# Expert rows of a graph layer: added to the output by the scatter itself, in place of a second pass over all rows

## The chip, the cores and the metric

The kernel runs on one core of one Trainium2 chip. The metric is device time in microseconds. The kernel before was run three times: 5855.3, 5860.06 and 5858.4 us, median 5858.4.

## The reference

A layer of a graph network over 6250 nodes of 256 features and 106,250 directed edges (50,000 in both directions and a loop on each node). Two hypergraph convolutions, linear attention and a mixture of experts are added up:

```
xn = layernorm(x)
x  = x + gnn(xn, src, dst) + mix(xn)          # gnn: 2 x (gather by src, sum by dst; gather by dst, sum by src)
xf = layernorm(x)
logits = (xf * gamma + beta) @ Wr + br        # 8 experts, the best 2 of each node
w = softmax(the two highest logits)
for e in range(8):
    h = gelu(xn_ffn @ W1[e] + b1[e]);  y_e = h @ W2[e] + b2[e]
    y = y + y_e * w_full[..., e]              # 0 unless e is one of the node's two
out = x + y
```

What the change touches is the last part: each node has two expert rows, each to be multiplied by its weight and added to the node's row of `x`.

## The kernel before

All tiles have 128 partitions; nodes lie in NB = 49 blocks of 128 rows (the last has 106). The program is written engine by engine, in order, with semaphores between the queues.

**Sorting and four passes.** Edges are sorted on the chip. Then four passes (`gather_pass`, L597, and `product_pass`, L1558) each gather 831 chunks of 128 rows from a table in DRAM by indirect DMA from GpSimd, multiply each chunk by a one-hot matrix `ohg` on TensorE and add the result to its block on VectorE (L1070). In `product_pass` TensorE waits, once for each group of four chunks, until as many gather groups have arrived as a number in a register says (`arrived`, L1540); SyncE counts arrivals (`s_arr`).

**The node stage.** `by_group` works through 12 groups of four blocks and one of a single block: second weights, residual, normalisation, logits and the two best experts. SyncE stores the normalised rows to `xf_d` (L509). The finished `x` stays in SBUF (`accs[1]`).

**Assigning rows to chunks.** 12,500 pairs of node and expert are placed in chunks of 128 rows of one expert each. VectorE computes both softmax weights (`wt`, L1299) early in this stage and only needs them at the end. The chunk table is made by 98 small matmuls; from it come, for each slot, the node's row `tok`, the row of the result `dest`, and for each chunk its expert `eid`. `s_ready` is raised by L1350.

**The expert loop.** NCE = 108 chunks, in a hardware loop of 27 turns with ER = 4 chunks each. For each chunk:
- VectorE copies the chunk's column of `tok` (L1360), and GpSimd gathers the rows from `xf_d` (L644), up to four chunks ahead.
- TensorE transposes them (L1734), ScalarE copies the result to `xT` (L801), TensorE multiplies by W1 (`up`, L1740), VectorE adds b1 (L1364), ScalarE applies the gelu (L805).
- TensorE transposes `h` (L1757), ScalarE copies it to `hT` (L814), TensorE multiplies by W2 (the down product, L1764), VectorE adds b2 (L1383).
- GpSimd scatters the 128 rows to `ye_d` in DRAM (L655), which has a row for each pair. Slots with no pair go to rows behind these.

TensorE's order is: transpose of `h` of c, transpose of the rows of c+2, up of c+1, down of c. PSUM and SBUF buffers are doubled, the rings of gathered rows and of results have four places.

**The closing stage.** SyncE waits for all scatters, then loads `ye_d` back in 13 loads (L531), two buffers in turn. VectorE multiplies each of the two rows of a node by its weight and adds it to `x` (L1392), ScalarE's queue writes the output (L822, L824).

Of the kernel before, what the change touches and what calls it, by code (L numbers as in the profile page):

```python
# [48 lines left out]
def gps_layer(nc, x, src, dst, gnn_w1, gnn_b1, gnn_w2, gnn_b2, gnn_a, wqkv, wout, bout,  # L49
# [68 lines left out]
    NCE = -(-((2 * N + NE * (P - 1)) // P) // ER) * ER  # L118
# [10 lines left out]
    with ctx:  # L129
# [21 lines left out]
        xf_d = dram("xf_d", (NB * P, F))  # L151
        ye_d = dram("ye_d", (2 * NB * P + NCE * P, F))
# [78 lines left out]
        def column(o, f, c):  # L231

            if o == 0:
# [34 lines left out]
                    for at in (0, KT * 2 * INNER + 2 * PAIRS * F)]  # L268
# [15 lines left out]
        fs = sb("fs", [P, 800], f32)  # L284
# [3 lines left out]
                        "tok": ((NCE + ER,), i32), "dest": ((NCE,), i32),  # L288
                        "eid": ((NCE + ER,), i32), "tokb": ((ER,), i32), "destb": ((ER,), i32)})

        fb_ = carve(ohg_flat, {"pos": ((NK,), f32), "run": ((NK,), f32), "oh": ((NK,), f32), "chunk": ((NK,), f32),
                               "slot": ((NK,), f32), "ti": ((2, NK), i32), "code": ((NK,), i32), "w": ((4, NB), f32),
                               "wt": ((2, NB), f32), "val": ((NK,), f32), "code16": ((NK,), u16), "cnt": ((NE,), f32), "nch": ((NE,), f32), "nchi": ((2, NE), i32),
# [4 lines left out]
                               "dummy": ((NCE,), f32), "none": ((NCE,), f32), "a": ((NCE,), f32), "v": ((NCE,), f32),  # L298
                               "v16": ((NCE,), f16), "vi": ((NCE,), i32)})

        fe = carve(gbuf_flat, {"xg": ((ER, F), f32), "h": ((2, H), f32), "hT": ((2, H), f32), "y": ((ER, F), f32)})
        xT = carve(ohg_flat, {"xT": ((2, F), f32)})["xT"]
        yl = [gbuf_flat[:, n * 2 * G * F:(n + 1) * 2 * G * F].rearrange("p (b j f) -> p b j f", b=G, j=2) for n in range(2)]
# [32 lines left out]
         s_it, s_t1e, s_c1, s_up, s_b1, s_ge, s_t2, s_c2, s_dn, s_b2, s_yfreed, s_add, s_od) = [sem(n) for n in (  # L336
             "s_gt s_gtc s_u s_z s_v1 s_d1 s_fold s_shift s_xf s_xfd s_xfree s_xft s_xftc s_lg s_lgc "
             "s_ei s_ed s_ex s_ecnt s_etot s_eoh s_eused s_esort s_iw s_ready "
             "s_it s_t1e s_c1 s_up s_b1 s_ge s_t2 s_c2 s_dn s_b2 s_yfreed s_add s_od").split()]
        s_fl = [sem(f"s_fl{n}") for n in range(2)]  # L340
        s_ys = [sem(f"s_ys{k}") for k in range(ER)]
        s_yl = [sem(f"s_yl{k}") for k in range(2)]
# [54 lines left out]
        def _(sp):  # L397
# [108 lines left out]
            def store(q, par, n):  # L506
                sp.wait_ge(s_xf, q + 1)
                settle(sp)
                sp.dma_start(rows(xf_d, q * G, n), xh[par][:, 0:n, :]).then_inc(s_xfd, 16)  # L509
                sp.wait_ge(s_xfd, (q + 1) * 16)  # L510
                sp.sem_inc(s_xfree, 1)
# [5 lines left out]
            sp.sem_inc(s_yfreed, ER)  # L517
            with sp.Fori(0, NCE // ER) as i:
                for k in range(ER):
                    sp.wait_ge(s_ys[k], i * 16 + 16)  # L520
                    sp.sem_inc(s_yfreed, 1)
            for k in range(ER):
                sp.wait_ge(s_g[k], XG0 + 16 * (NCE // ER + 1))
            sp.wait_ge(s_ge, NCE + 1)

            for q in range(NG + 1):
                n = G if q < NG else 1
                m = P if q < NG else LAST
                if q >= 2:
                    sp.wait_ge(s_add, q - 1)  # L530
                sp.dma_start(yl[q % 2][0:m, 0:n, :, :], ye_d[q * G * 2 * P:q * G * 2 * P + n * 2 * m, :].rearrange("(b p j) f -> p b j f", p=m, j=2)).then_inc(s_yl[q % 2], 16)  # L531
# [4 lines left out]
        def _(pool):  # L536
# [101 lines left out]
            gp.iota(fd["dummy"], pattern=[[P, NCE]], base=2 * NB * P + 1, channel_multiplier=1, allow_small_or_imprecise_dtypes=True).then_inc(s_iw, 1)  # L638


            def gather(k, count):
                pool.wait_ge(s_it, count)
                settle(pool)
                gp.indirect_dma_start(fe["xg"][:, k, :], None, xf_d, bass.IndirectOffsetOnAxis(sm["tokb"][:, k:k + 1], 0)).then_inc(s_g[k], 16)  # L644
# [3 lines left out]
            for k in range(ER):  # L648
                gather(k, k + 1)
            with pool.Fori(0, NCE // ER) as i:  # L650
                for k in range(ER):
                    gather(k, i * ER + (ER + k + 1))
                    pool.wait_ge(s_b2, i * ER + (k + 3))
                    settle(pool)
                    gp.indirect_dma_start(ye_d, bass.IndirectOffsetOnAxis(sm["destb"][:, k:k + 1], 0), fe["y"][:, k, :], None).then_inc(s_ys[k], 16)  # L655
# [3 lines left out]
        def _(act):  # L659
# [139 lines left out]
            def copy_x(k, count):  # L799
                act.wait_ge(s_t1e, count)  # L800
                A(xT[:, k % 2, :], PS[:, k % 2, 0:F], ACT.Copy).then_inc(s_c1, 1)  # L801

            def gelu(k, count):
                act.wait_ge(s_b1, count)
                A(fe["h"][:, k % 2, :], fe["h"][:, k % 2, :], ACT.Gelu).then_inc(s_ge, 1)  # L805

            act.wait_ge(s_ready, 1)
            copy_x(0, 1)
            gelu(0, 1)
            copy_x(1, 2)  # L810
            with act.Fori(0, NCE // ER) as i:
                for k in range(ER):
                    act.wait_ge(s_t2, i * ER + (k + 1))
                    A(fe["hT"][:, k % 2, :], PS[:, 4 + k % 2, :], ACT.Copy).then_inc(s_c2, 1)  # L814
                    copy_x(k, i * ER + (k + 3))
                    gelu(k + 1, i * ER + (k + 2))


            for q in range(NG + 1):
                act.wait_ge(s_add, q + 1)  # L820
                if q < NG:
                    act.dma_start(rows(out, q * G, G), accs[1][:, q * G:(q + 1) * G, 0:F]).then_inc(s_od, 16)  # L822
                else:
                    act.dma_start(out[q * G * P:N, :], accs[1][0:LAST, q * G, 0:F]).then_inc(s_od, 16)  # L824
            act.wait_ge(s_od, 16 * (NG + 1))
# [3 lines left out]
        def _(dve):  # L829
# [468 lines left out]
            link(V.reciprocal(wt[:, 0, :], w[:, 2, :]))  # L1298
            link(TT(wt[:, 1, :], wt[:, 0, :], w[:, 1, :], ALU.mult))  # L1299
# [35 lines left out]
            dve.wait_ge(s_iw, 2)  # L1335
            v = fd["v"]
            link(V.tensor_copy(fd["v16"], PS[:, 1, 0:NCE]))
            link(V.tensor_copy(fd["vi"], fd["v16"].bitcast(u16)))
            link(TS(v, fd["vi"], float(-LOWEST), 0.0, ALU.add, ALU.max))
            link(TS(fd["none"], v, 0.0, None, ALU.is_equal))  # L1340
            link(V.memset(sm["tok"], 0))
            link(STT(out=fd["a"], in0=v, scalar=-1.0, in1=fd["none"], op0=ALU.add, op1=ALU.add))
            link(V.tensor_copy(sm["dest"], fd["a"]))
            link(TS(sm["tok"][:, 0:NCE], sm["dest"], 1, None, ALU.logical_shift_right))
            link(TT(fd["dummy"], fd["dummy"], fd["none"], ALU.mult))
            link(STT(out=sm["dest"], in0=v, scalar=-1.0, in1=fd["dummy"], op0=ALU.add, op1=ALU.add))
# [7 lines left out]
            def experts_of(i):  # L1354
                return nc.values_load_multi_w_load_instructions(
                    sm["eid"][0:1, ds(i * ER, ER + 1)], engines=(DVE,), min_val=0, max_val=NE - 1,
                    skip_runtime_bounds_check_because="computed on the chip as a minimum with NE - 1")[1]

            def token_numbers(k, w):
                V.tensor_copy(sm["tokb"][:, k:k + 1], sm["tok"][:, ds(w, 1)]).then_inc(s_it, 1)  # L1360

            def add_b1(k, count, e):
                dve.wait_ge(s_up, count)
                TT(fe["h"][:, k % 2, :], PS[:, 2 + k % 2, :], fa_["b1r"][:, ds(e, 1), :].rearrange("p a f -> p (a f)"), ALU.add).then_inc(s_b1, 1)  # L1364

            dve.wait_ge(s_fw2, 32)
            for k in range(ER):
                token_numbers(k, k)
            e0 = nc.values_load_multi_w_load_instructions(
                sm["eid"][0:1, 0:1], engines=(DVE,), min_val=0, max_val=NE - 1,  # L1370
                skip_runtime_bounds_check_because="computed on the chip as a minimum with NE - 1")[1][0]
            add_b1(0, 1, e0)
            with dve.Fori(0, NCE // ER) as i:
                es = experts_of(i)
                for k in range(ER):
                    w_ = i * ER + k
                    dve.wait_ge(s_t1e, w_ + 1)
                    token_numbers(k, w_ + ER)
                    add_b1(k + 1, w_ + 2, es[k + 1])
                    dve.wait_ge(s_yfreed, w_ + 1)  # L1380
                    V.tensor_copy(sm["destb"][:, k:k + 1], sm["dest"][:, ds(w_, 1)])
                    dve.wait_ge(s_dn, w_ + 1)
                    TT(fe["y"][:, k, :], PS[:, 6 + k % 2, 0:F], fr["b2r"][:, ds(es[k], 1), :].rearrange("p a f -> p (a f)"), ALU.add).then_inc(s_b2, 1)  # L1383


            for q in range(NG + 1):
                n, m = (G, P) if q < NG else (1, LAST)
                dve.wait_ge(s_yl[q % 2], 16 * (q // 2 + 1))
                for j in range(2):
                    for b in range(n):  # L1390
                        x2 = accs[1][0:m, q * G + b, 0:F]
                        a = STT(out=x2, in0=yl[q % 2][0:m, b, j, :], scalar=wt[0:m, j, q * G + b:q * G + b + 1], in1=x2,  # L1392
                                op0=ALU.mult, op1=ALU.add)
# [395 lines left out]
```

## Time and profile before

| | us |
|---|---|
| median of three runs | 5858.4 |
| the profiled execution | 5866.34 |
| its span, first to last instruction | 5864.6 |
| PE busy | 4113.0 (70%) |
| DVE busy | 3605.1 (61%) |
| ACT busy | 1255.1 (21%) |
| POOL busy | 3860.7 (66%) |
| mean granted TensorE clock | 0.868 |

The busy shares are averages over stages with different limits. The four passes lie between about 650 and 5006 us, the node stage and the assignment between there and 5320, the expert loop from 5321 to 5787, the closing stage behind it. All times below are us from the span's start. Matmul ends are modelled. The clock is given as a share of full speed.

### The profile page before, as it was taken

What the parts mean: (1) busy time and instruction counts of PE and PEld (TensorE: products, weight loads), DVE (VectorE), ACT (ScalarE), POOL (GpSimd) and SP (SyncE); (2) the same over time, 40 slices, a digit from 0 to 9 for tenths busy, and PEclk for the clock granted to TensorE, in tenths of its full rate; (3) what the DMA queues carried; (4) which work ended last, traced back from release to release, by engine and by line L of the source; (5) the groups of instructions that cost most, each with busy time, mean ns of one, the idle gap of its engine ahead of it and who ended that gap; (6) DMA issues with size and microseconds to landing.
All of it is one profiled execution on the core that took longest, in us unless ns stands there. A gap on an engine that the chain in (4) does not pass through costs nothing.

```text
span 5864.6 us, 68260 instructions
## 1 busy us (share of the span) xinstructions
PE 4113.0 (70%) x16858; PEld 2694.3 (46%) x16859; DVE 3605.1 (61%) x11329; ACT 1255.1 (21%) x3285; POOL 3860.7 (66%) x3972
## 2 busy tenths in 40 slices
PE   4799799999975776777465555555566555557994
PEld 2555466665643444444344334333434434444662
DVE  7788788888876666566755554574555554454324
ACT  0388455555520000000100000000000000222331
POOL 2777777777776777777477777767777777003442
PEclk9899899999998999999787887887787777768997
DMA  3400233333334333333344444444333333411125
GB/s 123 133 2 2 59 100 102 102 100 101 100 104 137 112 112 112 113 112 111 112 139 136 136 140 137 136 143 142 105 105 106 105 105 105 134 53 41 63 64 161
DMA packets 322692, 616.69 MB, mean 105 GB/s; under 512 B 79716, under 2 KB 199096, under 8 KB 321848
## 3 DMA queue, kind: packets, MB, share of 16 engines
q0 software_dynamic: 182400, 464.97, 27.8%
q1 hardware_dynamic: 127932, 133.60, 6.9%
q10 hardware_dynamic: 12028, 14.28, 0.7%
q8 instruction: 137, 2.24, 0.2%
q14 instruction: 195, 1.60, 0.1%
HBM read 525.55 MB, written 87.01 MB: 104 GB/s over the span
## 4 chain that ended last, share of the span: by engine, by line
PE 40%; DVE 15%; DMA 14%; issue 10%; POOL 8%; SPq 1%; ACT 1%; DVEq 1%; ACTq 0%; PEldq 0%; POOLq 0%; PEld 0%
PE PS L1558 19%; POOL rowset L597 8%; PE PS L1482 7%; DVE rowset L1070 7%; DMA rowset<-table,idx 7%; PE PS L1740 3%; PE PS L1764 3%; PE PS L1596 3%; DMA region<-xn_d 2%; DMA skip_d<-region 2%; DVE ohg L1079 2%; PE PS L1634 2%; DMA region<-xt_d 1%; PE PS L1757 1%; DMA rowset<-ye_d 1%
## 5 line engine op out<-in xcount | busy, mean ns | idle before, releaser
L597 POOL DMA_INDIRECT rowset<-table,idx x3324 | 3206.0, 964 | 1088.3 <-issue 706.1
L1558 PE MATMUL PS<-rowset,ohg 128*128 x7040 | 2074.4, 437 | 925.1 <-issue 335.0
L1070 DVE TENSOR_TENSOR rowset<-rowset,PS 128x257 f32 (+1 forms) x3520 | 1478.0, 420 | 1482.0 <-PE PS L1558 1461.5
L1558 PEld LDWEIGHTS PS<-rowset,ohg 128*128 128x128 f32 x7040 | 1436.8, 215 | 1567.7 <-issue 1358.7
L1079 DVE TENSOR_SCALAR ohg<-iota,dl 128x128 f32<-128x128 f16 x2640 | 793.9, 301 | 91.7 <-issue 91.7
L1482 PE MATMUL PS<-region 128*128 128x416 f16 x3328 | 653.3, 339 | 0.0
L605 POOL DMA_INDIRECT scattered_d<-rowset x384 | 372.2, 969 | 132.9 <-issue 121.3
L1482 PEld LDWEIGHTS PS<-region 128*128 128x128 f16 x3328 | 324.5, 98 | 256.9 <-issue 0.9
L692 ACT ACTIVATE region<-region 128x128 f16<-128x128 f16 x832 | 334.1, 402 | 453.9 <-DVE region L994 431.7
L993 DVE TENSOR_SCALAR region<-iota_c,region 128x832 f16<-128x832 f16 x832 | 380.5, 457 | 22.9 <-issue 22.7
L693 ACT ACTIVATE region<-region 128x128 f16<-128x128 f16 x832 | 321.0, 386 | 0.0
L1482 PE MATMUL PS<-rowset,region 128*128 128x416 f16 x1792 | 320.3, 340 | 0.0
L1596 PE MATMUL PS<-region 128*128 128x512 f32 x392 | 234.8, 730 | 117.0 <-DMA region<-xt_d 117.0
L761 ACT ACTIVATE region<-region 128x8 f32<-128x8 f32 x2 | 0.5, 294 | 1377.8 <-PEq L1406 1377.8
L1634 PE MATMUL PS<-gmat,region 128*128 128x256 f32 x196 | 97.2, 648 | 246.1 <-DMA region<-xn_d 246.1
L993 DVE TENSOR_SCALAR rowset<-iota_c,region 128x832 f16<-128x832 f16 x448 | 227.4, 508 | 42.5 <-PE PS L1482 42.2
L1482 PEld LDWEIGHTS PS<-rowset,region 128*128 128x128 f16 x1792 | 174.6, 97 | 146.0 <-issue 2.1
L655 POOL DMA_INDIRECT ye_d<-rowset,fs x108 | 106.3, 984 | 199.4 <-DVE fs L1360 143.2
L725 ACT ACTIVATE region<-PS 128x1024 f32<-128x1024 f32 x49 | 50.1, 1023 | 842.2 <-PEq L1406 842.2
L994 DVE TENSOR_SCALAR region<-iota_h,region 128x128 f16<-128x128 f16 x832 | 214.5, 258 | 0.0
L1740 PE MATMUL PS<-region,ohg 128*128 x436 | 207.9, 600 | 0.0
L1764 PE MATMUL PS<-rowset 128*128 x864 | 204.1, 379 | 0.0
(322 smaller groups left out, 3530.2 us busy)
## 6 DMA issues: line engine op xcount, KB each, us to landing
rowset<-table,idx POOLq DMA_INDIRECT x3324, 2.8
table<-rowset SPq DMA_DIRECT2D x21, 896.0 KB, 5.1
region<-xt_d SPq DMA_DIRECT2D x98, 128.0 KB, 2.2
rowset<-ye_d SPq DMA_DIRECT2D x12, 1024.0 KB, 7.5
xpad_d<-rowset SPq DMA_DIRECT2D x1, 6272.0 KB, 20.7
xn_d<-rowset SPq DMA_DIRECT2D x49, 128.0 KB
xt_d<-rowset SPq DMA_DIRECT2D x49, 128.0 KB
table<-rowset SPq DMA_DIRECT2D x49, 128.0 KB
```

Source lines behind the costliest of these rows:

```text
L597: gp.indirect_dma_start(rowset[:, at + c % ring, 0:F], None, tables[p], bass.IndirectOffsetOnAxis(idx[p % 2][:, c:c + 1], 0)).then_inc(s_g ...
L605: gp.indirect_dma_start(scattered_d, bass.IndirectOffsetOnAxis(ln["place"][:, c:c + 1], 0), ln["edge"][:, c:c + 1], None).then_inc(s_sc[h] ...
L692: A(ohv[:, k % RING, 0, :], ohs[o][:, k % RING, :], ACT.Copy, scale=column(o, 2, c))
L693: A(ohv[:, k % RING, 1, :], ohs[o][:, k % RING, :], ACT.Copy, scale=column(o, 3, c)).then_inc(s_ohs[o], 1)
L993: TS(ohc[o][:, k % RING, :], iota_c[:, 0:NC], column(o, 0, c), None, ALU.is_equal)
L1070: TT(a, a, chunk_sum(p, k), ALU.add).then_inc(s_acc[p], 1)
L1079: m = TS(ohg[:, k % U, :], iota_1[:, :], dl[p % 2][:, i * U + k:i * U + k + 1], None, ALU.is_equal)
L1482: m = MM(PS[:, 2 * f + h, 0:HC], ohv[:, k % RING, f, :], ohc[o][:, k % RING, h * HC:(h + 1) * HC], start=False, stop=False)
L1558: m = MM(chunk_sum(p, k), ohg[:, k, :], rowset[:, ds(slot_of[k], 1), 0:width(p)].rearrange("p a f -> p (a f)"), start=True, stop=True)
L1596: MM(PS[:, h, :], mx["xt"][:, kt, :], mx["wkv"][:, kt, h * INNER:(h + 1) * INNER], start=kt == 0, stop=kt == KT - 1)
L1740: m = MM(PS[:, 2 + k % 2, :], xT[:, k % 2, kt * P:(kt + 1) * P], fr["w1"][:, ds(e, 1), kt, :].rearrange("p a f -> p (a f)"), start=kt == 0 ...
L1764: m = MM(PS[:, 6 + k % 2, 0:F], fe["hT"][:, k % 2, t * P:(t + 1) * P], fa_["w2"][:, ds(es[k], 1), t, :].rearrange("p a f -> p (a f)"), sta ...
```

## The change

- The second result buffer `ye_d` and the closing stage are gone.
- SyncE writes the finished `x` to `out` right behind the last store of `xf_d`, while rows are assigned to chunks.
- The rows of `xf_d` are two words longer (FW = 258), and SyncE writes both weights of each node there, from `wt`, now laid out as pairs. GpSimd's first gather waits for that. A gathered row brings both weights with it.
- VectorE picks the weight by whether the slot holds the node's first or second expert (`first`, `second`), in two operations per chunk. ScalarE multiplies the result by it, a fourth operation per chunk.
- GpSimd's scatter goes to `out` and adds. Slots with no pair have a row number beyond the last node and are left out. Since two chunks can hold the same node, each scatter waits until the one before has landed.
- The loop has 105 chunks and is written out; `tok` and `dest` are read in place, without the copies to `tokb` and `destb`. Expert numbers are read for 16 chunks at a time (17 registers) in place of four (5 registers).
- In `product_pass` the number of arrivals waited for is made at least 1 by one register operation for each group of four chunks (its declared minimum is 0 instead of 1).

```diff
-    NCE = -(-((2 * N + NE * (P - 1)) // P) // ER) * ER
+    NCE = (2 * N + NE * (P - 1)) // P
+    FW = F + 2
...
-        xf_d = dram("xf_d", (NB * P, F))
-        ye_d = dram("ye_d", (2 * NB * P + NCE * P, F))
+        xf_d = dram("xf_d", (NB * P, FW))
...
             by_group(sp, load, lambda q, par, n: None, store)
...
-            for k in range(ER):
-                sp.wait_ge(s_g[k], XG0 + 16 * (NCE // ER + 1))
-            sp.wait_ge(s_ge, NCE + 1)
-            for q in range(NG + 1):
-                n = G if q < NG else 1
-                m = P if q < NG else LAST
-                if q >= 2:
-                    sp.wait_ge(s_add, q - 1)
-                sp.dma_start(yl[q % 2][0:m, 0:n, :, :], ye_d[...]).then_inc(s_yl[q % 2], 16)
+            for q in range(NG + 1):
+                if q < NG:
+                    sp.dma_start(rows(out, q * G, G), accs[1][:, q * G:(q + 1) * G, 0:F]).then_inc(s_od, 16)
+                else:
+                    sp.dma_start(out[q * G * P:N, :], accs[1][0:LAST, q * G, 0:F]).then_inc(s_od, 16)
+            sp.wait_ge(s_wts, 1)
+            sp.dma_start(xf_d[:, F:FW].rearrange("(b p) j -> p b j", p=P), fb_["wt"]).then_inc(s_wtd, 16)
+            sp.wait_ge(s_od, 16 * (NG + 1))
             for k in range(ER):
+                sp.wait_ge(s_ys[k], 16 * -(-(NCE - k) // ER))
...
+            def gather(c):
+                if c >= ER:
+                    pool.wait_ge(s_t1e, c - ER + 1)
+                    pool.wait_ge(s_wsel, c - ER + 1)
+                gp.indirect_dma_start(fe["xg"][:, c % ER, :], None, xf_d, bass.IndirectOffsetOnAxis(sm["tok"][:, c:c + 1], 0)).then_inc(s_g[c % ER], 16)
...
+            pool.wait_ge(s_wtd, 16)
+            for c in range(ER):
+                gather(c)
+            pool.wait_ge(s_od, 16 * (NG + 1))
+            for c in range(NCE):
+                if c + ER < NCE:
+                    gather(c + ER)
+                pool.wait_ge(s_scl, c + 1)
+                if c:
+                    pool.wait_ge(s_ys[(c - 1) % ER], 16 * ((c - 1) // ER + 1))
+                gp.indirect_dma_start(out, bass.IndirectOffsetOnAxis(sm["dest"][:, c:c + 1], 0), fe["y"][:, c % ER, :], None,
+                                      bounds_check=N - 1, oob_is_err=False, compute_op=ALU.add).then_inc(s_ys[c % ER], 16)
...
+            for c in range(NCE):
+                act.wait_ge(s_t2, c + 1)
+                A(fe["hT"][:, c % 2, :], PS[:, 4 + c % 2, :], ACT.Copy).then_inc(s_c2, 1)
+                if c + 2 < NCE:
+                    copy_x(c + 2)
+                if c + 1 < NCE:
+                    gelu(c + 1)
+                act.wait_ge(s_b2, c + 1)
+                A(fe["y"][:, c % ER, :], fe["y"][:, c % ER, :], ACT.Copy, scale=sm["wsel"][:, 1, c % ER:c % ER + 1]).then_inc(s_scl, 1)
...
+            def weights(c):
+                at = c % ER
+                dve.wait_ge(s_t1e, c + 1)
+                if c >= ER:
+                    dve.wait_ge(s_scl, c - ER + 1)
+                link(TS(sm["wsel"][:, 0, at:at + 1], fe["xg"][:, at, F + 1:FW], sm["second"][:, c:c + 1], None, ALU.mult))
+                STT(out=sm["wsel"][:, 1, at:at + 1], in0=fe["xg"][:, at, F:F + 1], scalar=sm["first"][:, c:c + 1],
+                    in1=sm["wsel"][:, 0, at:at + 1], op0=ALU.mult, op1=ALU.add).then_inc(s_wsel, 1)
...
+                weights(c)
+                if c + 1 < NCE:
+                    add_b1(c + 1, es[c % U + 1])
+                if c >= ER:
+                    dve.wait_ge(s_ys[c % ER], 16 * (c // ER))
+                dve.wait_ge(s_dn, c + 1)
+                TT(fe["y"][:, c % ER, :], PS[:, 6 + c % 2, 0:F], fr["b2r"][:, ds(es[c % U], 1), :].rearrange("p a f -> p (a f)"), ALU.add).then_inc(s_b2, 1)
...
                         if k % IB == 0:
-                            pe.wait_ge(s_arr[p], arrived[k // AG])
+                            pe.reg_alu(at_least, pe.to_reg(arrived[k // AG]), 1, ALU.max)
+                            pe.wait_ge(s_arr[p], at_least)
```

GpSimd's queue in the expert loop, before: gathers of `xf_d` and scatters to `ye_d` in turn, the gather behind VectorE's copy of the row numbers (`s_it`), the scatter behind VectorE's bias add (`s_b2`).

```order
L644 DMA rowset<-xf_d,fs 128x256 [waits s_it]
L653 REGISTER_ALU
L655 DMA ye_d<-rowset,fs 26368x256 [waits s_b2]
L642 REGISTER_ALU
L644 DMA rowset<-xf_d,fs 128x256 [waits s_it]
```

The same place in the changed kernel, from the first gather on. `s_wtd` is the store of the weights, `s_od` the writes of `out`, `s_scl` ScalarE's scale, `s_ys0` to `s_ys3` the landings of scatters.

```order
L636 DMA rowset<-xf_d,fs 128x258 [waits s_wtd,s_xfree,s_ready]
L636 DMA rowset<-xf_d,fs 128x258 x3
L636 DMA rowset<-xf_d,fs 128x258 [waits s_wsel,s_t1e,s_od]
L650 DMA out<-rowset,fs 6250x256 [waits s_scl]
L636 DMA rowset<-xf_d,fs 128x258 [waits s_wsel,s_t1e]
L650 DMA out<-rowset,fs 6250x256 [waits s_ys0,s_scl]
L636 DMA rowset<-xf_d,fs 128x258 [waits s_wsel,s_t1e]
L650 DMA out<-rowset,fs 6250x256 [waits s_ys1,s_scl]
```

The order of gathers and scatters is kept; each scatter but the first has gained the wait for the landing of the one before it, and it waits for ScalarE instead of VectorE.

ScalarE's queue in the expert loop, before: copy of `hT` (L814), of `xT` (L801), gelu (L805).

```order
L811 ISA
L814 ACTIVATE rowset<-PS 128x512 [waits s_t2]
L800 REGISTER_ALU
L801 ACTIVATE ohg<-PS 128x256 [waits s_t1e]
L804 REGISTER_ALU
L805 ACTIVATE rowset<-rowset 128x512 [waits s_b1]
L814 ACTIVATE rowset<-PS 128x512 [waits s_t2]
```

The same place in the changed kernel (L809, L797 and L801 are the same three operations).

```order
L809 ACTIVATE rowset<-PS 128x512 [waits s_t2]
L797 ACTIVATE ohg<-PS 128x256 [waits s_t1e]
L801 ACTIVATE rowset<-rowset 128x512 [waits s_b1]
L815 ACTIVATE rowset<-rowset,fs 128x256 [waits s_b2]
L809 ACTIVATE rowset<-PS 128x512 [waits s_t2]
```

The scale L815, which waits for the bias add behind the down product of c, stands ahead of the copy of `hT` of chunk c+1.

## Rows read from the trace of the kernel before

**Rows 1.** Windows: length, busy us by engine (instructions), granted clock, DMA share, GB/s.

```profile
5500.00:5600.00 100.00, 100.00 (x435) 67.58 (x434) 30.31 (x97) 36.14 (x73) 46.71 (x48) 1.00 0.20 63
5800.00:5865.00 65.00, 0.00 (x0) 0.00 (x0) 35.81 (x86) 0.00 (x0) 0.00 (x0) 0.50 0.78 262
```

**Rows 2.** The chain that ended last, from 5770 on: start us, us, what.

```profile
5776.64 1.73 PE PS L1764 x8
5780.80 1.74 PE PS L1764 x8
...
5783.17 3.13 issue
...
5786.52 2.45 DMA ye_d<-rowset,fs
...
5789.35 5.32 DMA rowset<-ye_d
```

**Rows 3.** Timeline, the last DMA issued.

```profile
5860.20 0.28 ACTq L824 DMA_DIRECT2D out<-rowset  x1
```

**Rows 4.** Timeline in the expert loop: start us, us, engine, line [idle before, releaser].

```profile
5504.69 0.38 ACT L801 ACTIVATE ohg<-PS 128x256 f32<-128x256 f32 x1
...
5505.51 0.19 PEld L1764 LDWEIGHTS PS<-rowset 128*128 128x128 f32 x1 [0.24 <-issue]
5505.93 1.89 PE L1764 MATMUL PS<-rowset 128*128 x8
...
5506.25 0.69 DVE L1364 TENSOR_TENSOR rowset<-PS,rowset 128x512 f32<-128x512 f32 x1 [1.95 <-PE PS L1740]
5506.36 0.96 POOL L644 DMA_INDIRECT rowset<-xf_d,fs  x1 [0.30 <-issue]
...
5507.66 0.66 PE L1757 MATMUL PS<-ident,rowset 128*128 128x128 f32 x4
5507.98 0.42 DVE L1383 TENSOR_TENSOR rowset<-PS,region 128x256 f32<-128x256 f32 x1 [0.98 <-PE PS L1764]
...
5508.36 0.60 ACT L814 ACTIVATE rowset<-PS 128x512 f32<-128x512 f32 x1 [0.75 <-PE PS L1757]
...
5509.23 0.99 POOL L655 DMA_INDIRECT ye_d<-rowset,fs  x1 [1.91 <-DVE fs L1360]
```

**Rows 5.** Timeline ahead of the expert loop: the weights, the last preparation, the first gather.

```profile
5264.25 0.21 DVE L1299 TENSOR_TENSOR ohg<-ohg 128x49 f32<-128x49 f32 x1
...
5320.01 0.22 DVE L1350 TENSOR_SCALAR fs<-rowset 128x112 int32<-128x112 f32 x1
...
5321.34 0.97 POOL L644 DMA_INDIRECT rowset<-xf_d,fs  x1 [6.42 <-DVE fs L1360]
```

**Rows 6.** SyncE's DMAs by line (ns min/median/max, first and last start), then by issue.

```profile
L509 SPq DMA_DIRECT2D xf_d<-rowset x13: 345/396/406, 5043.5 to 5250.7; - x13
...
DMA to landing us min/median/max: 1.7/3.1/3.6
...
L490 SPq DMA_DIRECT2D region<-in_L_ffn_Wr x1: 613/613/613, 3965.5 to 3965.5; - x1
...
L492 SPq DMA_DIRECT2D region<-in_L_ffn_beta x1: 2526/2526/2526, 3968.3 to 3968.3; - x1
...
xpad_d<-rowset SPq DMA_DIRECT2D x1, 6272.0 KB, 20.7
```

**Rows 7.** DMA issues from 5345 to 5760: count, median us from issue to landing.

```profile
rowset<-xf_d,fs POOLq DMA_INDIRECT x100, 2.8
ye_d<-rowset,fs POOLq DMA_INDIRECT x100, 2.4
```

**Rows 8.** By line: TensorE's queue in the passes, and GpSimd's gathers, 700 to 1740 us.

```profile
L1535 PEldq TENSOR_LOAD <-blk_row x220: 1101/1104/1769, 659.5 to 4985.3; - x110
...
L1558 PEldq FUSED_REGOPS  x3520: 46/46/46, 665.5 to 5003.6; - x196
...
L597 POOL DMA_INDIRECT rowset<-table,idx x791 | 799.4, 1011 | 241.0 <-issue 171.8 <-DVE rowset L1070 69.1
```

More of the change, by code:

```diff
@@ L283, in gps_layer @@
         NK = 2 * NB
-        fs = sb("fs", [P, 800], f32)
+        fs = sb("fs", [P, 900], f32)
         sm = carve(fs, {"inv": ((G,), f32), "stats": ((G, 6), f32), "mv": ((G, 2), f32), "rstd": ((5, G), f32), "nega": ((1,), f32),
@@ L508, in store @@
                 settle(sp)
-                sp.dma_start(rows(xf_d, q * G, n), xh[par][:, 0:n, :]).then_inc(s_xfd, 16)
+                sp.dma_start(xf_d[ds(q * G * P, n * P), 0:F].rearrange("(b p) f -> p b f", p=P), xh[par][:, 0:n, :]).then_inc(s_xfd, 16)
                 sp.wait_ge(s_xfd, (q + 1) * 16)
@@ L637, in _ @@
             gp.iota(fd["iw"], pattern=[[1, NCE + ER]], base=0, channel_multiplier=0, allow_small_or_imprecise_dtypes=True).then_inc(s_iw, 1)
[L638 to L644, printed above, removed]
+            def gather(c):
[3 more added lines that the diff above has]
+                gp.indirect_dma_start(fe["xg"][:, c % ER, :], None, xf_d, bass.IndirectOffsetOnAxis(sm["tok"][:, c:c + 1], 0)).then_inc(s_g[c % ER], 16)
             pool.wait_ge(s_ready, 1)
             pool.wait_ge(s_xfree, 2 + NG + 1)
[L648 to L655, printed above, removed]
+            pool.wait_ge(s_wtd, 16)
[10 more added lines that the diff above has]
+                                      bounds_check=N - 1, oob_is_err=False, compute_op=ALU.add).then_inc(s_ys[c % ER], 16)
         @block.scalar
@@ L796, in _, with copy_x, gelu @@
             A(fb_["w"][:, 1, :], fb_["w"][:, 0, :], ACT.Exp).then_inc(s_ex, 1)
[L799 to L805, printed above, removed]
-            act.wait_ge(s_ready, 1)
[L808 to L825, printed above, removed]
+            def copy_x(c):
+                act.wait_ge(s_t1e, c + 1)
+                A(xT[:, c % 2, :], PS[:, c % 2, 0:F], ACT.Copy).then_inc(s_c1, 1)
+            def gelu(c):
+                act.wait_ge(s_b1, c + 1)
+                A(fe["h"][:, c % 2, :], fe["h"][:, c % 2, :], ACT.Gelu).then_inc(s_ge, 1)
+            act.wait_ge(s_ready, 1)
+            copy_x(0)
+            gelu(0)
+            copy_x(1)
+            for c in range(NCE):
[7 more added lines that the diff above has]
+                A(fe["y"][:, c % ER, :], fe["y"][:, c % ER, :], ACT.Copy, scale=sm["wsel"][:, 1, c % ER:c % ER + 1]).then_inc(s_scl, 1)
         @block.vector
@@ L1362, in add_b1 @@
-            def add_b1(k, count, e):
-                dve.wait_ge(s_up, count)
-                TT(fe["h"][:, k % 2, :], PS[:, 2 + k % 2, :], fa_["b1r"][:, ds(e, 1), :].rearrange("p a f -> p (a f)"), ALU.add).then_inc(s_b1, 1)
-            dve.wait_ge(s_fw2, 32)
[L1367 to L1383, printed above, removed]
@@ L1386, in _, with add_b1 @@
[L1386 to L1393, printed above, removed]
-                    if j == 0:
-                        link(a)
-                a.then_inc(s_add, 1)
+            def add_b1(c, e):
+                dve.wait_ge(s_up, c + 1)
+                TT(fe["h"][:, c % 2, :], PS[:, 2 + c % 2, :], fa_["b1r"][:, ds(e, 1), :].rearrange("p a f -> p (a f)"), ALU.add).then_inc(s_b1, 1)
@@ new lines, in _ @@
+            dve.wait_ge(s_fw2, 32)
+            for c in range(NCE):
+                if c % U == 0:
+                    es = experts_of(c)
+                if c == 0:
+                    add_b1(0, es[0])
+                weights(c)
[5 more added lines that the diff above has]
+                TT(fe["y"][:, c % ER, :], PS[:, 6 + c % 2, 0:F], fr["b2r"][:, ds(es[c % U], 1), :].rearrange("p a f -> p (a f)"), ALU.add).then_inc(s_b2, 1)
```

109 lines of the change are left out of this document (51 added, 58 removed).

## The prediction

> **What bounds the kernel now.** I read the busy shares of the last stretches first, then the chain of work that ended last, then one turn of the expert loop instruction by instruction, and last the DMA landings. The windows show two regimes. From 5500 to 5600 us TensorE is busy 100.00 of 100 us at clock 1.00. From 5800 to the end TensorE, ScalarE and GpSimd do nothing, VectorE is busy 35.81 of 65 us and the DMA engines 0.78 [rows 1]. That is the closing stage, in which the expert rows come back from `ye_d`, are weighted, added and written. The chain says where it begins: the last down product ends at 5780.80 + 1.74 = 5782.54, the last scatter goes out at 5786.52 and lands at 5788.97, and the first of 13 loads of `ye_d` starts at 5789.35 [rows 2]. The span is 5864.6, so 75.6 us lie behind the last landing. The last DMA is issued at 5860.20 [rows 3], 4.4 us before the end.
>
> The expert loop turns in 4.16 us per chunk: the down product starts at 5776.64 and again at 5780.80 [rows 2]. All its PE work is back to back.
>
> **What goes.** The closing stage, and three chunks: 3 x 4.16 = 12.5 us. The 3.13 us of issue ahead of the last scatter [rows 2] are mostly a hitch of that one turn, since a scatter normally starts 0.83 us behind VectorE (5507.98 + 0.42 = 5508.40, then 5509.23) [rows 4].
>
> **What comes at the loop's start.** VectorE's last preparation ends at 5320.23, the first gather starts at 5321.34 because four copies stand between [rows 5]. They go, and GpSimd starts 0.83 behind: 5321.06. A second iota that VectorE waited for goes too, and one small operation of the chain: together I take 0.6 us earlier, within 0 and 1.
>
> The new gate on that gather is the store of the weights. The last store of `xf_d` is issued at 5250.7 [rows 6]; those stores land in 1.7 us at the least [rows 6], so the 13 writes of `out` start at about 5253. The 6.3 MB store of rows of 1 KB landed in 20.7 us, so they drain by about 5274 [rows 6]. The weights themselves are ready at 5264.46 [rows 5]. Behind the writes stands one DMA of 128 x 49 = 6272 pieces of 8 bytes. The nearest rows are two loads of 256 small pieces each: SyncE was held 613 ns by one and 2526 ns by the other [rows 6], 2.4 and 9.9 ns a piece, so 15 to 62 us, landing at 5289 to 5336. I take 25 us, which is near the shorter (the longer stood behind megabytes of other loads): it lands near 5300, 20 us before it is needed. The upper end costs 16 us.
>
> The Trainium skill ("DMA: Bandwidth & Descriptors", section "Rules for kernel authors") says that a non-contiguous last dimension becomes one descriptor per element; pairs of 8 bytes are close to that case, and by it this small store is as dear as 6272 pieces. The trace of before has no such store.
>
> **The loop, engine by engine.** TensorE's matmuls are the same, so its floor stays 4.16 us. ScalarE gets a fourth operation, scale 128x256. It stands behind the gelu and ahead of the next copy of `hT`, and waits for VectorE's bias add, which ends at 5508.40. The copy would have started at 5508.36 [rows 4]. The nearest ScalarE row of that width takes 0.38 us (128x512: 0.60) [rows 4]; I take 0.42. So the scale runs 5508.45 to 5508.87 and the copy 5508.90 to 5509.50. The weight load that needs it starts one period behind 5505.51, at 5509.67 [rows 4]: 0.17 us are left. Cost 0; if the scale took 0.60, or the wait more, up to 0.3 x 104 = 31 us. VectorE's two 128x1 operations need less than 0.22 each (a 128x112 one takes 0.22 [rows 5]) and fall in its idle time ahead of the next b1 add (1.95 us before 5506.25 [rows 4]), where a copy went out: 0.
>
> GpSimd is where the change can hurt. Scatter c now waits for the landing of scatter c-1 as well as for the scale, and behind it in the queue stands the gather of c+5, for which TensorE has chunks of reserve. A plain scatter lands 2.4 us after it starts (2.45 in the chain), and GpSimd starts 0.83 behind its release. The gather (0.30 + 0.96) [rows 4] fits in the flight. So the serial chain turns in 2.45 + 0.83 = 3.28 us with a plain write; 4.16 - 3.28 = 0.88 us is the room for what the adding costs, which I call x.
>
> x is in no row of before. From below: 0, if reading the old rows overlaps with all else. From near: a gather, which reads DRAM, lands in 2.8 us and a scatter in 2.4 [rows 7], so a DRAM read adds 0.4; and the DMA engines are busy 0.20 of the time on one gather and one scatter per turn [rows 1], 0.83 us, so 0.42 us for another 128 rows: x = 0.8. From above: a whole gather's flight ahead of the write, 2.8 - 0.96 = 1.84, and the building of the descriptors twice as long, + 0.98 [rows 4]: x = 2.8. I take 0.8, since the two reads have no cause to wait for each other: the chain turns in 4.1 us, just under TensorE's 4.16.
>
> The Trainium skill ("Collectives: The Full Stack", section "The bandwidth ceiling: the fold count and why AG ≠ RS ≠ AR") says that an adding DMA is slow because it reads two sources and not because of the addition, and measured half a copy's rate. By it the data part of a scatter doubles, which is the 0.42 above; no row of before shows it.
>
> **Register work.** Each group of four chunks in the four passes gets one more register operation on TensorE's queue: 880 x 46 ns = 40 us if nothing hid it [rows 8]. It stands behind the wait for the one-hots and ahead of the wait for arrivals. The gathers set the pace even in the first pass, where TensorE is busiest: 791 gathers take 799.4 us and the 241.0 us between them are the same 0.30 us that lies between any two [rows 8], so GpSimd never waits for TensorE: 0. Expert numbers are read 17 at a time, 7 times, instead of 5 at a time. A read of 16 in the passes takes 1.10 us [rows 8], and TensorE was 100% busy across such reads every four chunks: 0.
> By the Trainium skill ("Runtime: NRT & Kernel Launch", section "Instruction fetch mechanics") a register read costs about 200 ns per register, thus 3.4 us a read; beyond a down product's 1.73 us it would stall TensorE 1.7 us six times, 10 us. The trace's 1.10 us for 16 speaks against it.
>
> **The sum.** Last down product ends 5782.54 - 12.5 - 0.6 = 5769.4. VectorE's add: + 0.15 + 0.44 = 5770.0; scale + 0.47; GpSimd + 0.83 = 5771.3; landing + 2.45 + 0.8 = 5774.6. The end: 4.4 us behind the last issue of before, of which 1.7 was landing if the 106 rows took the least that a store of `xf_d` does [rows 6], so + 2.7 = 5777.3. That is 87.3 us under the span of 5864.6. The profiled execution took 5866.34, 7.9 over the median of 5858.4; carried over to the median: 5858.4 - 87.3 = 5771.
>
> **The rivals.** What a run of this kernel can tell from no change is 0.2%, 11.7 us.
> - Forecast, 0.48: x up to 0.88, the chain of scatters hides behind TensorE. 5771, by itself 5762 to 5780 (start, end, a few tenths per turn).
> - The scatters set the pace, but less than the tail gives back, 0.25: x = 1.3, 4.58 us a turn, 104 x 0.42 = 44 us more: 5815. For it: 0.08 us of room is little. Against: nothing else is on the DMA engines.
> - Slower than before, 0.22: the wait of scatter c for the landing of scatter c-1. It decides from x = 1.83 on: (87.3 + 11.7) / 104 = 0.95 over 4.16. With x = 2.8 the turn is 6.08 us, 104 x 1.92 = 200 us more: 5971. For it: the rows would be read, added and written in series, 8 per DMA engine. Against: gathers of the passes land in 2.8 us with several in flight.
> - The chain hides, but the weights land late (+16) or ScalarE's order holds up TensorE (+31), 0.05: 5787 to 5802. That ScalarE has only 0.17 us left speaks for it.
>
> No change within 0.2% needs x between 1.61 and 1.83: 0.05, taken out of the second. Faster: 0.48 + 0.20 + 0.05 = 0.73; slower 0.22. The range runs from 5762 to 5900 (a turn of 5.4 us, x = 2.1), which leaves out about 0.05 below and 0.14 above.
>
> **What will show it.** Right: down products 4.16 us apart and TensorE at 100%; adding scatters landing in under 3.3 us from their start; first gather near 5320.7; the last scatter near 5771 and the end some 6 us behind; register work without a trace in the gather rate. Wrong: the bias add of chunk c waiting for a DMA, TensorE idle each turn, scatters back to back with their landings (the second and third case); GpSimd waiting at the first gather for the weights' store; TensorE waiting for ScalarE's copy of `hT`.

## The result: 0.27% faster where 1.5% was forecast

The changed kernel took 5851.4 us (median of 15 runs, 5841.9 to 5862.4), the kernel before, run beside it, 5864.5 us (5855.3 to 5872.7). The ratio is 0.9973, 95% interval 0.9967 to 0.9980. That is 13 us less between the medians and 16 by the ratio, where 87 were forecast. The changed kernel's profiled execution took 5854.1 us, its span is 5851.6 at a mean clock of 0.870.

The closing stage is gone as forecast; the expert loop gave most of it back. First the windows, with the columns of [rows 1].

```profile
5500.00:5600.00 100.00, 90.82 (x376) 57.93 (x375) 30.20 (x84) 39.96 (x84) 53.60 (x42) 1.00 0.34 54
...
5800.00:5851.00 51.00, 35.10 (x146) 22.75 (x145) 12.10 (x33) 15.42 (x31) 21.83 (x17) 0.93 0.25 34
```

TensorE's full 100 us have become 90.82, and GpSimd issues 42 DMAs instead of 48 in the same time. The loop turns more slowly. The scatter's own line says why: ns min/median/max and first and last start, then what GpSimd's idle time ahead of it ended with (us, times), then the landing.

```profile
L650 POOL DMA_INDIRECT out<-rowset,fs x105: 1554/1586/1652, 5347.4 to 5842.8; - x105
...
  DMA out<-rowset,fs: 157.4, 85
...
  ACT rowset L815: 36.5, 15
...
DMA to landing us min/median/max: 2.7/3.8/4.9
```

An adding scatter keeps GpSimd for 1.59 us where the plain one took 0.99 [rows 4], and lands 3.8 us behind its start instead of 2.4 [rows 7]. The profile puts 85 of 105 waits down to a DMA of the scatter's own kind, the landing of the scatter before. From first to last start there are 495.4 us, over 104 turns 4.764 us each, against 4.16. Two turns in the chain (start us, us, what):

```profile
5506.23 0.52 ACT rowset L815
5506.75 0.12 issue
5506.88 3.91 DMA out<-rowset,fs
...
5510.90 0.55 issue
...
5511.67 3.89 DMA out<-rowset,fs
```

The scatter's landing takes 3.91 us, and the next one starts 0.88 us behind it. The timeline shows how TensorE comes to wait (start us, us, engine, line [idle before, releaser]):

```profile
5501.56 0.51 ACT L815 ACTIVATE rowset<-rowset,fs 128x256 f32<-128x256 f32 x1 [1.25 <-DVE rowset L1375]
...
5502.17 1.59 POOL L650 DMA_INDIRECT out<-rowset,fs  x1 [2.71 <-ACT rowset L815]
...
5504.06 0.98 POOL L636 DMA_INDIRECT rowset<-xf_d,fs  x1 [0.30 <-issue]
...
5506.87 0.44 PE L1716 MATMUL PS<-ident,rowset 128*128 128x128 f32 x2 [0.83 <-DMA rowset<-xf_d,fs]
5506.88 1.59 POOL L650 DMA_INDIRECT out<-rowset,fs  x1 [1.84 <-ACT rowset L815]
5508.77 0.98 POOL L636 DMA_INDIRECT rowset<-xf_d,fs  x1 [0.30 <-issue]
```

Each gather stands behind a scatter in GpSimd's queue. As the scatters fall back, so do the gathers; after the reserve of some chunks is used up, TensorE's transpose of the rows (L1716) waits for a gather, 61.4 us in all between 5380 and 5820:

```profile
POOL out L650 <- DMA out<-rowset,fs: 135.7, 74, 2.2
...
PEld PS L1716 <- DMA rowset<-xf_d,fs: 61.4, 85, 2.4
```

The rows that name `ACT rowset L815` as a scatter's releaser, at 5502.17 and 5506.88 and in the chain, are put down wrongly. There are 105 scales and 105 scatters, in the same order, so they can be paired by counting. The scatter at 5506.88 is the 34th, and its scale, also the 34th, ended at 5502.08 (the row of 5501.56), 4.8 us earlier; the scale that ended at 5506.75 belongs to the next scatter. What ended 0.88 us before 5506.88 is the landing of the scatter of 5502.17. Counted so over the whole loop, no scatter but the first starts within 1.3 us of the end of its own scale (median 4.3 us), and 94 of 104 start 0.88 us behind the landing before. In the scatters' chain there is nothing else: the 495.4 us are 399.8 of flights, start to landing, and 95.7 from a landing to the next start. The lag behind the own scale grows from 0.85 us at the first chunk to 5.1 at the ninth, and that is the reserve being used up.

The end of the program: the last scatter and GpSimd's drain, changed kernel.

```profile
5842.82 1.55 POOL L650 DMA_INDIRECT out<-rowset,fs  x1 [1.99 <-DMA out<-rowset,fs]
```

```profile
L130 POOLq DRAIN  x1: 8798/8798/8798, 5842.6 to 5842.6; - x1
```

The last scatter landed at 5845.52. The drain lasts until 5851.40, 7.0 us beyond the end of that instruction, and every engine waits for it. The same drain in the kernel before took 2.9 us and ended at 5789.3, in the shadow of the closing stage:

```profile
L129 POOLq DRAIN  x1: 2926/2926/2926, 5786.4 to 5786.4; - x1
```

**The account against the forecast span of 5777.3.** 74.3 us are to be found. The 104 turns are 495.4 - 432.9 = 62.5 us longer. The first scatter starts at 5347.4 where 5771.3 - 432.9 (104 x 4.162) = 5338.4 was forecast: 9.0. From the last scatter's start to the end there are 8.8 us where 5.95 were forecast: 2.9.

### The profile page after: what moved, and what is told of

Its sections match the earlier page's. It is cut to its first block, busy times and chain, and to the rows that moved or that the text cites. A ratio compares the mean times of both kernels' runs of the same rounds, so it can differ in the third digit from the quotient of the medians.

```text
span 5851.6 us, 67858 instructions
## 1 busy us (share of the span) xinstructions
PE 4131.0 (71%) x16796; PEld 2689.7 (46%) x16796; DVE 3583.2 (61%) x11213; ACT 1292.3 (22%) x3378; POOL 3922.4 (67%) x3961
## 4 chain that ended last, share of the span: by engine, by line
DMA 22%; PE 22%; POOL 15%; DVE 15%; issue 12%; DVEq 1%; ACT 1%; SPq 1%; ACTq 0%; POOLq 0%; PEldq 0%; PEld 0%
POOL rowset L590 15%; PE PS L1540 12%; DMA rowset<-table,idx 10%; DVE rowset L1060 7%; DMA out<-rowset,fs 6%; PE PS L1461 4%; PE PS L1578 2%; DMA region<-xn_d 2%; DMA skip_d<-region 2%; PE PS L1616 2%; DVE ohg L1069 1%; DMA region<-xt_d 1%; PE PS L1673 1%; DVE ohg L1064 1%; DVEq L1060 0%
## 5 line engine op out<-in xcount | busy, mean ns | idle before, releaser
L650 POOL DMA_INDIRECT out<-rowset,fs x105 | 166.5, 1586 | 206.6 <-DMA out<-rowset,fs 157.4
L1351 DVE TENSOR_TENSOR rowset<-PS,rowset 128x512 f32<-128x512 f32 x105 | 72.7, 693 | 227.7 <-PE PS L1722 227.7
```

## The experiments

Kernels beside which the same time of the kernel before stands shared a chip.

**The changed kernel again**, for the same chip as the next three (before: 5874.9 us there).

> The changed kernel again, beside the runs of before that the next three kernels share. Both theories on the loop expect 0.997 of before. Of the 13 us by which its passes ended later in the profile: if they belong to the kernel, the last gather of the passes ends near 5013 again and pass 0 takes about 1101 us again; if they are scatter between executions, the last gather ends anywhere from 4998 to 5014.

Measured 5862.0 us, ratio 0.9978 (0.9969 to 0.9987): the result stands. In its profile the first pass takes 1101.0 us and the last gather of the passes ends at 5012.2, much as in the first profile of this kernel (1101.5 and 5013.6).

**The adding taken out of the scatter.** The sum is left out: rows overwrite each other.

```diff
-  bounds_check=N - 1, oob_is_err=False, compute_op=ALU.add)
+  bounds_check=N - 1, oob_is_err=False)
```

> The changed kernel with a scatter that overwrites in place of one that adds (the sum is left out); all waits, the row filter, the scale and the order stay. Theory: the added cost of the adding DMA, 1.35 us of landing, sets the turn; without it the chain of scatters turns in about 3.3 us, the loop falls back to TensorE's 4.16 us, the scatter lands in 2.45 us and the kernel takes 60 us less than the changed one (about 5790). Rival, ScalarE's fourth operation and its order set the turn: it stays at 4.7 us and the time at 5851. Rival, the filter of row numbers is the cost: GpSimd's instruction stays at 1.59 us and about half of the gain is missing (turn near 4.2 to 4.3).

Measured 5801.6 us, ratio 0.9869 (0.9854 to 0.9885), 60 us under the changed kernel beside it. The window and the scatter's line:

```profile
5500.00:5600.00 100.00, 99.34 (x429) 66.80 (x427) 34.96 (x96) 45.41 (x96) 47.24 (x49) 1.00 0.21 62
```

```profile
L650 POOL DMA_INDIRECT out<-rowset,fs x105: 983/1017/1035, 5359.7 to 5793.6; - x105
...
  ACT rowset L815: 182.9, 95
...
DMA to landing us min/median/max: 2.1/2.5/3.5
```

With every wait left in place, the plain write takes 1.02 us, lands in 2.5, and seldom holds up the next: the releaser is ScalarE 95 times (97 scatters start 0.8 us behind their own scale, paired by counting), and the turn is (5793.6 - 5359.7) / 104 = 4.172 us. So it takes the price of adding to slow the loop; the wait for a landing, ScalarE's fourth operation and the longer rows don't do it without that. The price has two parts: 1.59 - 1.02 = 0.57 us for the instruction, and (3.8 - 1.59) - (2.5 - 1.02) = 0.73 us behind it.

**Two targets in turn.** Even chunks are added into `out`, odd ones into a second tensor, so a scatter waits only for the last but one. The final sum of the two is left out.

```diff
-  if c:
-      pool.wait_ge(s_ys[(c - 1) % ER], 16 * ((c - 1) // ER + 1))
-  gp.indirect_dma_start(out, ...
+  if c >= 2:
+      pool.wait_ge(s_ys[(c - 2) % ER], 16 * ((c - 2) // ER + 1))
+  gp.indirect_dma_start((out, out2)[c % 2], ...
```

> The changed kernel with two target tensors: even chunks add to the output, odd chunks to a second tensor that starts with the same rows (the final sum of the two is left out), so that a scatter waits for the landing of the one before the last. Theory, the wait for the neighbour's landing sets the turn and nothing else: adding scatters still take 1.59 us on GpSimd and land in 3.8 us, yet the loop turns in 4.16 to 4.2 us, TensorE is at 100% and the time is about 5800 where the changed kernel has 5862 on that chip (ratio to before 0.987). Rival, the adding itself is the limit (reads of DRAM, the DMA engines): the turn stays above 4.6 us and the landings grow beyond 4 us as two overlap.

Measured 5789.8 us beside 5859.7 of the kernel before, ratio 0.9874 (0.9857 to 0.9890).

```profile
5500.00:5600.00 100.00, 100.00 (x435) 67.43 (x434) 35.10 (x97) 45.60 (x97) 62.17 (x49) 1.00 0.40 63
```

```profile
L656 POOL DMA_INDIRECT out<-rowset,fs x105: 1555/1587/1652, 5361.0 to 5794.3; - x105
...
DMA to landing us min/median/max: 2.7/3.8/4.4
```

The adding scatter is as long as ever (1.59 and 3.8 us), yet TensorE is at 100 of 100 and the turn 4.167 us. The length of the scatter does harm only through the wait for the neighbour's landing.

**Without the row filter.** Slots with no pair add into rows behind the nodes of a scratch tensor, so that no row is filtered (`bounds_check` gone). Expert rows don't reach the output.

```diff
-  gp.indirect_dma_start(out, ..., bounds_check=N - 1, oob_is_err=False, compute_op=ALU.add)
+  gp.indirect_dma_start(acc_d, ..., compute_op=ALU.add)
```

> The changed kernel adding into a scratch tensor that has rows for the empty slots, so that no filter of row numbers is needed (the output is left without its expert rows). Theory, the adding makes the longer building of descriptors, not the filter: 1.55 to 1.59 us as in the changed kernel, turn 4.7 us, time within 5 us of the changed one; the three chunks at the end, mostly empty slots, no longer turn faster (3.5 to 3.9 before), which costs 2 to 3 us. Rival, filter and adding together make it: the instruction falls by 0.1 us or more and the turn with it, 10 us over the loop.

Measured 5841.2 us beside 5859.7, ratio 0.9967 (0.9957 to 0.9977).

```profile
L656 POOL DMA_INDIRECT acc_d<-rowset,fs x105: 1554/1586/1644, 5342.9 to 5830.0; - x105
...
DMA to landing us min/median/max: 3.6/3.8/5.3
```

The instruction stays at 1.59 us, so its 0.57 us are the adding's. The turn is not quite the same, and here the rival was right in part: it is 4.684 us on average (487.1 us over the loop) against 4.764 (495.4). In the chain of this run:

```profile
5558.43 3.83 DMA acc_d<-rowset,fs
...
5563.04 3.83 DMA acc_d<-rowset,fs
```

The next scatter starts at 5563.04, 0.78 us behind the landing at 5562.26, where it takes 0.88 with the filter (both are the usual value of their runs). The filter brings a register move ahead of each scatter (`L650 POOLq MOVE` x105), which this kernel doesn't have. So the filter costs no flight and no instruction time of the adding scatter, but about 0.1 us of its start, some 10 us over the loop, part of which the last chunks give back: with the filter, chunks of empty slots land in 2.7 us. A plain scatter took 0.99 us before and 1.02 above; the two differ in their target as well.

**The wait only where it is needed.** Within one expert no node comes twice, so neighbouring chunks can share a node only where the expert changes. SyncE waits for the last but one always, for the last with a number computed on the chip (`need`: 16 more where the expert changes), and then releases GpSimd.

```diff
+  link(TT(fd["chg"], fd["ew"][:, 1:NCE + 1], fd["ew"][:, 0:NCE], ALU.not_equal))
+  link(STT(out=sm["need"], in0=fd["chg"], scalar=16.0, in1=fd["iy"][:, 0:NCE], op0=ALU.mult, op1=ALU.add))
...
+  for c in range(1, NCE):                                   # SyncE
+      if c >= 2:
+          sp.wait_ge(s_ys[(c - 2) % ER], 16 * ((c - 2) // ER + 1))
+      if c > ER:
+          sp.reg_alu(landed_before, sp.to_reg(need[(c - ER - 1) % U]), 1, ALU.max)
+          sp.wait_ge(s_ys[(c - 1) % ER], landed_before)
+      else:
+          sp.wait_ge(s_ys[(c - 1) % ER], 16 * ((c - 1) // ER + 1))
+      sp.sem_inc(s_go, 1)
...
-  pool.wait_ge(s_ys[(c - 1) % ER], 16 * ((c - 1) // ER + 1))
+  pool.wait_ge(s_go, c)
```

> The changed kernel, but a scatter waits for the landing of the one before it only where the expert changes (two chunks of one expert hold no node twice), and always for the one before that; SyncE does the waiting, against a number computed with the chunk table, and releases GpSimd. Theory: 98 of 104 turns fall to TensorE's 4.16 us, 60 us less than the changed kernel, ratio to before 0.987 (0.986 to 0.990). Rival, TensorE's turn was bound by the gathers that stand behind the scatter in GpSimd's queue and not by the wait: turn above 4.5 us, and a gain of less than 20 us.

Measured 5787.9 us beside 5859.7, ratio 0.9877 (0.9860 to 0.9893): 72 us less than before, with the whole output computed.

```profile
5500.00:5600.00 100.00, 99.80 (x431) 67.00 (x431) 34.94 (x96) 45.28 (x96) 62.16 (x49) 1.00 0.40 63
```

```profile
L668 POOL DMA_INDIRECT out<-rowset,fs x105: 1552/1588/1649, 5343.8 to 5777.3; - x105
...
  SPq L538: 20.3, 11
...
DMA to landing us min/median/max: 2.7/3.8/4.2
```

11 of 104 waits are put down to SyncE's release, where in the changed kernel all 104 scatters started behind a landing; the turn is 4.168 us. In the timeline two adding scatters stand closer than a landing:

```profile
5499.38 1.59 POOL L668 DMA_INDIRECT out<-rowset,fs  x1 [2.09 <-issue]
...
5502.65 1.59 POOL L668 DMA_INDIRECT out<-rowset,fs  x1 [0.40 <-issue]
```

5502.65 is 3.27 us behind 5499.38. This form, which the changed kernel forbids itself, lets a late chunk catch up.

**The register operation.** The passes ended 13.3 us later than before, so it was put into the kernel before alone, and made five in the changed one.

```diff
-  pe.wait_ge(s_arr[p], arrived[k // AG])
+  pe.reg_alu(at_least, pe.to_reg(arrived[k // AG]), 1, ALU.max)
+  pe.wait_ge(s_arr[p], at_least)
```

> The kernel before with the one register operation per group of four chunks and nothing else of the change. If register work is what the passes lost: 10 to 15 us more than before, ratio 1.002, and the last gather of the passes ends near 5013. If gathers set the pace and it is hidden: ratio 1.000 within 0.001, last gather near 5000, and each of the four passes within 2 us of before.

> The changed kernel with five register operations in place of one for each of the 880 groups. If they lie on the path: 4 x 880 x 46 ns = 160 us more than the changed kernel. If gathers set the pace: the same time as the changed kernel in passes 1 to 3, and at most a few us in pass 0 where TensorE is 95% busy.

One operation in the kernel before: 5882.1 us beside 5874.9, ratio 1.0014 (1.0005 to 1.0023). Five in the changed kernel: 5861.2 us, ratio 0.9980 (0.9971 to 0.9989), the same as with one (0.9978). One costs about 7 us, four more nothing. With one, the last gather of the passes ends at 5019.2. On another chip (before: 5865.8 us) one and five were put into the kernel before side by side.

> The kernel before with one register operation per group, a second time, on another chip, beside the kernel with five. If the 0.14% belong to it: 1.0010 to 1.0018 again. If it was scatter between executions: within 0.001 of 1. The last gather of the passes then ends wherever pass 0, with its number of long gathers, puts it.

> The same with five operations per group. On the slow chip this was 0.9999 of before, with 0.9987 to 1.001 as interval. If the time of the operations counts at all, it is above the kernel with one by up to 4 x 880 x 46 ns = 160 us, ratio 1.03; if it is hidden, both kernels are equal within 0.001.

1.0011 (1.0000 to 1.0021) for one, 1.0010 (1.0001 to 1.0019) for five. So it isn't the time of the operations. The edit also lowers the declared minimum of the number, and no run parts this from the operation. Whether its place matters was asked on a chip where the kernel before took 7378.7 us, so only ratios can be read: the operation ahead of the wait for the one-hots, five of them in the old place, and the kernel with the wait at the change of expert with the early operation.

> The kernel before with the one register operation per group, placed ahead of the wait for the one-hots, so that the three waits of a group stand on one instruction again as before. If the parted waits made the 0.14% of the register operation alone, this is 1.000 of before within 0.001. If the operation itself did, it is 1.0014 again.

> The kernel before with five register operations per group. If each operation costs its 46 ns on the path, even a fifth of the time: 1.0014 + 0.0055 = 1.007. If what costs is only that there is an operation between the two waits, or the code around it: 1.0014 again. If the 0.14% of one operation was scatter of the executions: anywhere from 0.9995 to 1.002.

> The kernel that waits for the neighbour's landing only where the expert changes, with the register operation placed early. Loop as there (4.16 us a turn). If the placing counts: 0.9863 of before; if not: 0.9877 again.

Ratios 1.0007 (0.9994 to 1.0020), 0.9999 (0.9987 to 1.0011) and 0.9885 (0.9863 to 0.9906). The first two can't be told from each other, from no change, or from the 1.0010 above, and the third repeats the gain of 0.9877 on a slower chip. On this chip GpSimd's gathers waited 1080.2 us for VectorE's adds (305.2 in the kernel before), so another thing sets the pace there and the first two say little about the other chips. Place and mechanism of the operation stay open.

## Why the prediction was wrong, step by step

**The step that failed: x, the cost of adding, taken as 0.8 us.** It is 1.3 (0.57 + 0.73, by the run without adding) to 1.4 (3.8 - 2.4). The forecast took from the nearest rows only the reading of the old rows, and argued that "the two reads have no cause to wait for each other". It left the longer instruction (+ 0.98, there a part of the upper bound) out of the likeliest value. A part of either kind came: 0.57 us of a longer instruction, 0.73 behind it. The decision hung on 0.08 us of room between 4.08 and 4.16, and the case "x up to 0.88" was less than a third of the way from 0 to 2.8, so nothing in the rows carried a chance of 0.48. The chain is 3.8 + 0.88 = 4.7 us, the usual turn. Eight turns of 5.4 to 6.1 and four of 3.5 to 4.0 make the mean 4.764. Of the eight, four stand behind a landing that took 4.6 to 4.9 us, and in four the next scatter started 1.6 to 2.2 us behind the landing instead of 0.88; what caused either is open.

The second rival was the right one: x = 1.3, 4.58 us a turn, 5815. Its turn was still short by 0.18 us, 19 us over 104: half is the flight (3.84 on average against 3.75), half the start behind a landing (0.92 against 0.83). With the 9.0 ahead of the loop and the 2.9 at the end that makes 5846. The last 5 us are the carrying over: the profiled execution of before lay 7.9 us over the median used, that of the changed kernel only 2.7.

**The Trainium skill's rule on the adding DMA** ("Collectives: The Full Stack", section "The bandwidth ceiling: the fold count and why AG ≠ RS ≠ AR") puts the cost into reading two sources. The run without adding fits it in part: 0.73 us of 1.3 lie behind the instruction, where the prediction had 0.42 for the data, but 0.57 lie in the instruction itself, on GpSimd. No run parts the reading from the addition.

**The passes: register work at 0, measured about 7 us.** The gathers' rate was the argument. By line, GpSimd from 700 to 1740 us in the changed kernel, as in [rows 8]:

```profile
L590 POOL DMA_INDIRECT rowset<-table,idx x784 | 800.2, 1021 | 240.7 <-issue 179.5 <-DVE rowset L1060 61.2
```

784 gathers instead of 791 in the same time: in this stretch seven gathers, at 1040 / 791 = 1.31 us each 9 us, went missing. The idle time between gathers is 0.31 us as before (240.7 / 784), so GpSimd still doesn't wait for TensorE; the gathers themselves are longer, 1021 ns on average instead of 1011. Of the 13.3 us by which the last gather comes later, 1.3 lie ahead of the first pass, 6.4 in it (1101.5 us from first to last gather, against 1095.1), 1.6 in the third, 4.0 between passes. The second and fourth are equal to within 0.3 us. In the first pass some gathers start 2.3 us apart instead of 1.3: 33 of them before, 38 now, and 33 to 46 in the ten profiles with the operation on chips of the usual speed, whose first pass took 1098.2 to 1111.9 us. Of the kernel before there is only one such profile. So a part of the 13.3 us is chance of that execution; the ratios of the three runs that add only this to the kernel before (1.0014, 1.0011, 1.0010) give 6 to 8 us. That the gathers' rate hides all register work was thus wrong by a little: the rate itself fell. What stretches those few gathers isn't settled.

**The start.** The first gather, forecast near 5320.7, came 11.2 us later:

```profile
5331.47 0.22 DVE L1340 TENSOR_SCALAR fs<-rowset 128x109 int32<-128x109 f32 x1
...
5331.96 0.97 POOL L636 DMA_INDIRECT rowset<-xf_d,fs  x1 [5.45 <-DVE fs L1340]
```

13.3 us come from the passes. Behind them it was 2.7 us quicker than before, where 0.6 was forecast: GpSimd starts 0.27 us behind VectorE, not 0.83. From the first gather to the first scatter it took 15.4 us, where 17.7 were forecast, so of the 11.2 us 9.0 are left. The store of the weights did what was forecast:

```profile
5264.83 14.64 SPq L517 DMA_DIRECT2D out<-rowset  x12
...
5280.77 1.22 SPq L521 DMA_DIRECT2D xf_d<-ohg  x1
```

It landed at 5294.95, forecast near 5300, needed at 5332: 6272 pieces of 8 bytes within 14.2 us. The number is partly luck: the writes of `out` started at 5264.8 and not at 5253, and the small store took 14.2 us instead of 25.

**ScalarE's order held.** The scale takes 0.51 us, forecast 0.42, which uses 0.09 of the 0.17 us that were left:

```profile
L815 ACT ACTIVATE rowset<-rowset,fs x105: 509/510/513, 5346.0 to 5840.4; 128x256 f32<-128x256 f32 x105
```

Yet without the adding, TensorE is busy 99.34 of 100 us and the turn is 4.172 against 4.16 (1.2 us in all). So the fourth case did not come, and TensorE's floor stayed.

**The expert numbers at 0: held.** Seven reads of up to 17 registers, in the run without the adding, ns min/median/max:

```profile
L1709 PEldq TENSOR_LOAD <-fs x7: 844/1361/1371, 5343.4 to 5752.8; - x7
```

1.36 us (1.60 in the changed kernel) fit beneath a down product of 1.73, as 1.10 for 16 did. The estimate of 3.4 us from the Trainium skill ("Runtime: NRT & Kernel Launch", section "Instruction fetch mechanics") didn't come.

**The end** was forecast as 5.95 us behind the last scatter's start and took 8.8. The landing was not the last thing (2.70 us in this chunk of mostly empty slots); the drain was, 5.9 us behind it. The drain takes the same 8.80 us in all the kernels with 105 adding scatters, also without the filter, where the last scatter lands 3.87 us behind its start; it takes 9.78 us with plain ones and took 2.93 in the kernel before. So it doesn't follow the landing or the adding, and what sets it is open. The forecast carried a figure of ScalarE's queue over to GpSimd's.

**The third rival** (slower, x from 1.83) is refuted: x is 1.4. The wait for the neighbour's landing was the right mechanism, at half its price.

## What to carry to other kernels

- An adding scatter that must wait for its neighbour is a chain of its own: its instruction, its flight and the start behind a semaphore, here 4.7 us for 128 rows of 1 KB. Compare this with the loop's turn before replacing a separate pass by it, and if the two are within a few tenths, ask first whether the wait is needed each time; here nearly all of the loop's 62.5 us lay in waits between chunks that could not collide (ratio 0.9978 down to 0.9877, 59 us).
- Where a term decides by less than its bounds are apart, the forecast is a toss, and a number in the middle needs a row of its own before it may carry most of the chance.

## What the runs showed of the hardware

- The adding makes GpSimd's instruction 1.59 us instead of 1.02 and the landing 3.8 instead of 2.5 us, for 128 rows of 1 KB. Leaving out rows by their number adds nothing to that, but the scatter starts 0.88 us behind the landing that releases it instead of 0.78.
- GpSimd's drain ends 7.0 us beyond its last DMA instruction in the changed kernel, 5.9 behind the landing; in the kernel before it ended 1.8 and 0.4 us behind them. Its length (8.80, 9.78, 2.93 us) isn't explained.
- The store of 6272 pieces of 8 bytes held SyncE for 1.22 us, about as long as the 12 stores ahead of it (14.64 us in all), and landed 14.2 us behind its issue.
- One register operation between two waits of TensorE's queue, 880 times, came with 0.10 to 0.14% more time on two chips, five of them with no more than one. On a third, slower chip no difference shows.
